# Values of an attention kernel by one indirect gather per unit, with four neighbouring keys to a partition

## The chip, the core and the metric

The kernel runs on one core of a Trainium2 chip. The metric is the device time of the whole launch in microseconds (us); lower is better. Engines are named as the profile names them: PE is the tensor engine's matmul, PEld its weight load, DVE the vector engine, ACT the scalar engine, POOL the GpSimd engine, and SP the engine that issues most of the DMAs (DMAs are issued by ACT and POOL too).

## The reference, cut to what matters

Two layers are added to a residual stream `x` of 8 sequences of 128 tokens and 512 features. Layer 0 is one product per sequence with a weight picked by id. Layer 1 is attention over a paged cache.

```
x = x + einsum('bsi,boi->bso', x, weight[adapter_ids])         # layer 0
# layer 1: 8 sequences, 8 key heads, 4 query heads to a key head, D = 128
q, k, v = x @ Wq.T, x @ Wk.T, x @ Wv.T                          # q and k: RMS norm, rotary angles
kc = k_cache[block_table].reshape(bsz, 512, HK, D)              # 16 pages of 32 keys per sequence
vc = v_cache[block_table].reshape(bsz, 512, HK, D)
k_all, v_all = concat([kc, k]), concat([vc, v])                 # 512 cached keys + 128 new ones
valid_c = arange(512)[None, :] < cache_seqlens[:, None]
probs = softmax(where(valid, q @ k_all.T * SCALE, -1e30))
x = x + (probs @ v_all) @ Wo.T
```

The softmax and the product with the values sum over all keys, so the order in which a unit's 512 cached keys stand is free, as long as scores, mask and values use the same one.

## The kernel before

All of it is one program written by hand for five instruction streams that meet by semaphores; no scheduler orders anything. The work of layer 1 is cut into 64 **units** `u = 8 * hk + b`, one key head `hk` and one sequence `b` each. A unit projects queries (tile `Q`, 128x512), new keys and values (`KV`), turns them, forms the scores of four heads against 640 keys (`S`), takes the softmax, turns the probabilities, multiplies them with the values (`O`), and multiplies the result with the output weights (`Y`). Every fp32 operand is split into a high part (rounded to fp32r) and a low part (the rest), and each product is three matmuls: high x high, low x high, high x low. So each operand has a pair of tiles: `qh`/`ql`, `kh`/`kl` (keys), `vh`/`vl` (values), `wh`/`wl` (weights), `pth`/`ptl` (turned probabilities), `oh`/`ol` (outputs).

The units are pipelined. In **period** `i` the engines work on the scores of unit `i`, the projections of unit `j = i + 1`, the probabilities and values of unit `w = i - 1` and the output product of unit `o = i - 2`. The first loop (`i` from -1 to `NA` = 8) turns probabilities on PE. In the second loop (`i` from 9) they are written as two fp16 planes and turned by DMA transposes that SP issues (`turn_upper`, `turn_lower`).

POOL's stream in a period of the second loop is, in this order: `split_w(i, 0)` (a low part of a 128x512 chunk of weights, tile `wl`, if the table `LO_POOL` has one there), `keys_lo(j)` (tile `kl`), `q_sum(j)` (tile `m`, after DVE's products), `values_hi(w)` (`vh`), `scales(j)` (`var`, `rst`), `values_lo(w)` (`vl`), three `p_lo` (`ptl`), `split_w(i, 1)`, two more `p_lo`. Ten chunks of `wl` fall into eight periods: `LO_POOL` places them so that between two `q_sum` there are 2, 2, 0, 1, 1, 2, 2 and 0 of them, over and over. PE needs `q_sum(j)` for `turn_q(j)` and `p_lo(w, t)` for `times_v(w, t)`, and its own stream is in a fixed order as well.

The cache comes as one array `kv`, with 16 rows of heads (values in the even ones, keys in the odd ones) of 64 pages of 4096 numbers. There, a page of values is 32 keys of 128 numbers; a page of keys is 128 features of 32 keys. For the first nine units (`NL` = 9) keys are loaded page by page from `kv` (`load_kt`), and values by four indirect gathers on POOL (`gather_v`), each of which brings 128 rows of 512 bytes by the row numbers in `kidx` (`kidx1` for unit 8). Meanwhile SP and ACT copy the pages of the later units to `cache_rows` in DRAM, in the order of each sequence's table, 14 rows of heads to a page (12 for sequence 0; `copy_page`, lines 335 to 340; in the periods up to 13). From unit 9 on, `load_k` and `load_v` bring a unit's keys and values from there by one DMA each (lines 342 to 350, and 438 to 445):

```
e.wait_ge(g_vlo, v - 1 if v <= NA else v)
e.dma_start(rawv[raw_at(v)], copy[2 * hk, b].rearrange(
    "k (r d) -> (k r) d", d=D).rearrange("(t p) d -> p t d", p=P)
```

Key number `128 * t + p` stands in partition `p`, tile `t`. SP issues `load_v(i)` in period `i`, after the mask and the weights and ahead of `turn_upper(i, 0)`; it waits until `values_lo(i - 1)` has read the buffer. `keys_hi` (ACT, line 770) rounds the loaded keys into `kh`, `keys_lo` (POOL, line 609) subtracts that from them into `kl`; both read 512 numbers in a row. On DVE, `key_rows` and `key_rows_1` compute the row numbers of the gathers.

## Time and profile before

| | |
|---|---|
| time, median of 3 runs | 1002.83 us (1002.82 to 1006.3) |
| span of the profiled execution | 1006.6 us |
| PE busy | 994.3 us, 99% |
| DVE, ACT, POOL busy | 861.5 (86%), 810.3 (80%), 795.8 us (79%) |
| chain that ended last | PE 95%, DVE 2%, ACTq 1%, ACT 1%, issue 1% |
| moved by DMA | 180.94 MB, 105.45 MB of it read from HBM and 31.86 MB written |
| q1, the queue of most DMAs | 68.9% of the 16 engines |

The page gives no time of its own for the profiled execution beside its span; of the three times listed, the 1006.3 us is the one near it. A share of busy time is a mean over the whole span: the first loop (up to about 190 us) has another mix than the second. In the tables of the trace, a row with an arrow names the tile written and the tiles read, and the bracket at a row's end is how long the engine sat idle before it and what released it.

### The profile page before, as it was taken

The numbers are of one execution on the slowest core, as the hardware profiler recorded it, in microseconds if no ns is written. First come the engines' busy times: TensorE is split into PE (matmuls) and PEld (weight loads), VectorE is DVE, ScalarE is ACT, GpSimd is POOL, SyncE is SP. The second block draws the span as 40 slices with busy tenths as digits, with TensorE's granted clock in tenths as the row PEclk, the third lists the DMA queues.
The fourth block names the chain that finished last, engine by engine and source line by source line (L and its number), as shares of the span: only waits on it lengthen the run. The fifth ranks groups of instructions, "written<-read, shape, count | busy, mean of one in ns | idle before, by whom it ended". The sixth has DMA issues, their size and how long they took to land.

```text
span 1006.6 us, 19441 instructions
## 1 busy us (share of the span) xinstructions
PE 994.3 (99%) x5471; PEld 864.3 (86%) x5471; DVE 861.5 (86%) x1787; ACT 810.3 (80%) x2109; POOL 795.8 (79%) x811
## 2 busy tenths in 40 slices
PE   8999999999999999999999999999999999999998
PEld 6778888888888888888888888888888888888886
DVE  7676657799999899999998999899999999998995
ACT  4455456698889889888988898898888988988884
POOL 4876677497889879897898888898798978888672
PEclk9999999999999999999999999999999999999999
DMA  8999879899988888888988888888988879888873
GB/s 254 277 262 260 283 229 258 213 211 201 221 162 162 161 158 153 166 157 152 171 153 162 156 160 165 148 168 155 170 148 165 157 151 166 162 162 144 153 149 84
DMA packets 513643, 180.94 MB, mean 180 GB/s; under 512 B 429873, under 2 KB 495682, under 8 KB 513538
## 3 DMA queue, kind: packets, MB, share of 16 engines
q1 hardware_dynamic: 381280, 143.20, 68.9%
q10 hardware_dynamic: 131106, 34.15, 15.3%
q0 software_dynamic: 1152, 2.36, 0.8%
q8 instruction: 45, 0.74, 0.3%
q14 instruction: 60, 0.49, 0.2%
HBM read 105.45 MB, written 31.86 MB: 136 GB/s over the span
## 4 chain that ended last, share of the span: by engine, by line
PE 95%; DVE 2%; ACTq 1%; issue 1%; ACT 1%; another core or an unknown queue 0%; POOL 0%; DVEq 0%
PE S L1408 22%; PE O L1341 7%; PE O L1343 7%; PE O L1342 7%; PE Q L1341 6%; PE Q L1343 6%; PE Y L1341 6%; PE Q L1342 6%; PE Y L1343 6%; PE Y L1342 6%; PE T L1347 4%; PE KV L1342 3%; PE KV L1341 3%; PE KV L1343 3%; PE KV L1361 1%; PE Y L1361 1%
## 5 line engine op out<-in xcount | busy, mean ns | idle before, releaser
L1080 DVE SCALAR_TENSOR_TENSOR pr<-pr,rc,raw 128x640 f16<-128x640 f32 x220 | 258.8, 1177 | 15.3 <-ACT raw L817 8.3
L1052 DVE CUSTOM_DVE_ANT_0 pr<-S,mask,rst 128x640 f32<-128x640 f32 x256 | 225.4, 881 | 16.6 <-PE S L1408 13.3
L837 ACT ACTIVATE pr<-pr,nb 128x640 f32<-128x640 f32 x256 | 211.7, 827 | 14.5 <-DVE nb L1052 14.5
L817 ACT ACTIVATE raw<-pr,rc 128x640 f16<-128x640 f32 x220 | 176.2, 826 | 0.6 <-DVE rc L1068 0.4
L617 POOL TENSOR_TENSOR m<-m 128x512 f32<-128x512 f32 x63 | 112.5, 1786 | 73.7 <-DVE m L1119 69.8
L591 POOL TENSOR_SCALAR ptl<-first 128x512 fp32r<-128x512 f16 x140 | 111.8, 799 | 17.6 <-issue 6.0
L570 POOL TENSOR_TENSOR kl<-raw,kh 128x512 fp32r<-128x512 f32 x64 | 97.8, 1528 | 34.5 <-ACT kh L720 33.5
L1408 PE MATMUL S<-kh,qh 128*128 128x320 f32 x512 | 120.8, 317 | 3.7 <-DVE nb L1052 3.6
L591 POOL TENSOR_SCALAR ptl<-turned 128x512 fp32r<-128x512 f16 x135 | 108.3, 802 | 11.2
L1408 PE MATMUL S<-kh,ql 128*128 128x320 f32 x512 | 116.8, 309 | 0.0
L783 ACT ACTIVATE Q<-Q 128x128 f32<-128x128 f32 x256 | 68.2, 266 | 59.9 <-DVE m L1119 59.9
L1408 PE MATMUL S<-kl,qh 128*128 128x320 f32 x512 | 116.2, 308 | 0.0
L1408 PEld LDWEIGHTS S<-kh,qh 128*128 128x128 f32 x512 | 91.7, 189 | 23.8 <-issue 4.7
L1341 PE MATMUL O<-pth,vh 128*128 128x512 f32 x252 | 105.5, 419 | 0.8 <-DVE ptl L983 0.5
L1341 PE MATMUL Y<-wh,oh 128*128 128x512 f32 x252 | 104.7, 415 | 0.4 <-DVE ol L983 0.4
L1341 PE MATMUL Q<-wh,xh 128*128 128x512 f32 x256 | 101.5, 396 | 0.5 <-issue 0.5
L1343 PE MATMUL Q<-wh,xl 128*128 128x512 f32 x256 | 100.9, 394 | 0.0
L1342 PE MATMUL Q<-wl,xh 128*128 128x512 f32 x256 | 100.2, 391 | 0.0
L1342 PE MATMUL Y<-wl,oh 128*128 128x512 f32 x252 | 99.7, 395 | 0.0
L1343 PE MATMUL Y<-wh,ol 128*128 128x512 f32 x252 | 99.6, 395 | 0.0
L1343 PE MATMUL O<-pth,vl 128*128 128x512 f32 x252 | 99.2, 394 | 0.0
L1342 PE MATMUL O<-ptl,vh 128*128 128x512 f32 x252 | 98.6, 391 | 0.0
(179 smaller groups left out, 2674.9 us busy)
## 6 DMA issues: line engine op xcount, KB each, us to landing
wraw<-in_wall SPq DMA_DIRECT2D x74, 256.0 KB, 4.4
cache_rows<-in_kv ACTq DMA_DIRECT2D x80, 224.0 KB
raw<-cache_rows SPq DMA_DIRECT2D x57, 256.0 KB, 4.0
raw<-cache_rows ACTq DMA_DIRECT2D x53, 256.0 KB, 5.0
mask<-mask_rows SPq DMA_DIRECT2D x64, 128.0 KB
cache_rows<-in_kv SPq DMA_DIRECT2D x36, 224.0 KB
first<-in_lw SPq DMA_DIRECT2D x5, 1024.0 KB
cache_rows<-in_kv SPq DMA_DIRECT2D x16, 192.0 KB, 4.2
```

Of the source, the lines that this page charges most:

```text
L570: return e.tensor_tensor(dst, src, hi.bitcast(F32), ALU.subtract)
L591: e.tensor_scalar(ptl[:, i % 3, :].rearrange("p (g n) -> p g n", g=G), plane_tile(u, 1, t), 1.0 / PS, 1.0, ALU.mult, ALU.mult).then_inc(g_ ...
L617: e.tensor_tensor(m1[:, :, :], m1[:, :, :], m2[:, :, :], ALU.add).then_inc(q_added, 1)
L783: made = e.activation(part, part, ACT.Square, accum_out=ssq[:, j % 2, r:r + 1])
L817: e.activation(upper16[:, g, :], pr[:, slot(u, g), :], ACT.Copy, scale=rc[:, u % 2, g:g + 1]).then_inc(a_f1, 1)
L837: e.activation(pr[:, slot(u, g), :], pr[:, slot(u, g), :], ACT.Exp, bias=nb[:, u % 2, g:g + 1], scale=-1.0, accum_out=sm[:, u % 2, g:g + 1 ...
L1052: e.tensor_tensor_reduce(pr[:, slot(u, g), :].rearrange("p (a n) -> p a n", a=2), S[:, :, 0:320], mask[:, u % 2, :].rearrange("p (a n) -> ...
L1080: e.scalar_tensor_tensor(out=lower16(u, g), in0=pr[:, slot(u, g), :], scalar=rc[:, u % 2, g:g + 1], in1=upper16[:, g, :], op0=ALU.mult, op ...
L1341: e.matmul(dst, lh, rh, start=first, stop=False)
L1342: e.matmul(dst, lh, rl, start=False, stop=False)
L1343: return e.matmul(dst, ll, rh, start=False, stop=last)
L1408: made = e.matmul(S[:, a, 0:320], l[:, u % 2, qs], r[:, u % 2, 320 * a:320 * a + 320], start=first, stop=last)
```

## The change

The keys are laid out otherwise: four neighbouring keys stand in one partition. Partition `p` holds keys `4 * (p % 8)` to `4 * (p % 8) + 3` of the unit's page `p // 8`, and tile `t` holds the `t`-th of each four.

- **Values.** The array is split in two, `kc` and `vc`. In `vc` a row is four neighbouring keys, 512 numbers (2 KB). A unit's values are then 128 such rows, one to a partition, and one indirect gather brings them. `gather_v(v)` on POOL does so for all 64 units; `load_v` on SP is gone. In the first loop it stands behind `values_lo(i)`, one gather where there were four; in the second loop it stands at the end of POOL's period, behind `p_lo(w, 4)`, for unit `i`. `values_hi` waits for its semaphore.
- **Row numbers.** `kidx` has one number per partition and unit (64 columns); DVE computes them for one head at a time (`value_rows`), head 0 in the prologue, two heads in each of periods 1 to 3 and the last in period 4. The table comes by one DMA of 128x8 where there were four of 32x32.
- **Copies.** `cache_rows` holds keys alone: `copy_page` moves 7 rows of heads (6 for sequence 0) where it moved 14 (12). The number of copies and their places stay.
- **Keys.** A page of keys is stored with its 32 keys in the order (t, j), key `4 * j + t`. `keys_hi` and `keys_lo` read the loaded keys through a view (`by_tile`) whose runs are 8 numbers long, 64 of them, and write in the order (t, page, j). The mask's numbers (`iota`) stand in the same order.

```diff
-def build(nc, x, xt, lw, wall, kv, ids_lens, table, pages, qkw, consts, iota, out):
+def build(nc, x, xt, lw, wall, kc, vc, ids_lens, table, pages, qkw, consts, iota, out):
...
+        def by_tile(keys):
+
+            return keys.rearrange("d (g t j) -> d t g j", g=NPG, t=NT)
+
+        def tiles_of(keys):
+            return keys.rearrange("d (t g j) -> d t g j", g=NPG, t=NT)
...
-            rows = slice(2 if b >= NL - NB else 4, 2 * NK)
+            rows = slice(1 if b >= NL - NB else 2, NK)
             e.dma_start(copy[rows, b, k, :].rearrange("r (s n) -> s r n", s=16),
-                        kv[rows, bass.ds(number, 1), :].rearrange("r a (s n) -> (a s) r n", s=16)
+                        kc[rows, bass.ds(number, 1), :].rearrange("r a (s n) -> (a s) r n", s=16)
...
-            def load_v(v):
-                hk, b = divmod(v, NB)
-                if v < NL + NB:
-                    e.wait_ge(d_copy[b], 16 * NPG)
-                e.wait_ge(g_vlo, v - 1 if v <= NA else v)
-                e.dma_start(rawv[raw_at(v)], copy[2 * hk, b].rearrange(
-                    "k (r d) -> (k r) d", d=D).rearrange("(t p) d -> p t d", p=P)
-                            ).then_inc(d_v[v % 2], 16)
...
-                if NL <= i < NU:
-                    load_v(i)
...
-            def gather_v(v, t):
-                hk, b = divmod(v, NB)
-                if t == 0:
-                    e.wait_ge(c_kidx, 1)
-                    if hk == 1:
-                        e.wait_ge(c_kidx1, 1)
-                    if v >= 2:
-                        e.wait_ge(g_vlo, v - 1)
-                rows_of = (kidx, kidx1)[hk]
+            def gather_v(v):
+                e.wait_ge(c_kidx, v // NB + 1)
+                if v >= 2:
+                    e.wait_ge(g_vlo, v - 1 if v <= NA else v)
                 e.indirect_dma_start(
-                    out=rawv[raw_at(v)][:, t, :], out_offset=None,
-                    in_=kv.rearrange("c a (r d) -> (c a r) d", d=D),
-                    in_offset=bass.IndirectOffsetOnAxis(
-                        ap=rows_of[:, NT * b + t:NT * b + t + 1], axis=0)
+                    out=rawv[raw_at(v)].rearrange("p t d -> p (t d)"), out_offset=None, in_=vc,
+                    in_offset=bass.IndirectOffsetOnAxis(ap=kidx[:, v:v + 1], axis=0)
                 ).then_inc(d_rawv[v % 2], 16)
...
             def values_hi(u):
-                if u < NL:
-                    e.wait_ge(d_rawv[u % 2], 64 * (u // 2 + 1))
-                else:
-                    e.wait_ge(d_v[u % 2], 16 * ((u - NL) // 2 + 1))
+                e.wait_ge(d_rawv[u % 2], 16 * (u // 2 + 1))
...
-                minus(kl[:, j % 2, 0:512], rawk[raw_at(j)], kh[:, j % 2, 0:512]).then_inc(g_kc, 1)
+                minus(tiles_of(kl[:, j % 2, 0:512]), by_tile(rawk[raw_at(j)]),
+                      tiles_of(kh[:, j % 2, 0:512])).then_inc(g_kc, 1)
...
-                if 1 < j < NL:
-                    gather_v(j, 0)
-                    gather_v(j, 1)
+                if 1 < j <= NA:
+                    gather_v(j)
...
-                if 1 < j < NL:
-                    gather_v(j, 2)
-                    gather_v(j, 3)
...
+                if i < NU:
+                    gather_v(i)
...
-                rounded(kh[:, j % 2, 0:512], rawk[raw_at(j)]).then_inc(a_kc, 1)
+                rounded(tiles_of(kh[:, j % 2, 0:512]), by_tile(rawk[raw_at(j)])).then_inc(a_kc, 1)
...
-            for g in range(4):
-                e.dma_start(tabb[32 * g:32 * g + 32, :],
-                            table[g:g + 1, :].broadcast_to([32, NB * NT])).then_inc(d_tab, 16)
+            e.dma_start(tabb[:, :], table).then_inc(d_tab, 16)
...
-                if i == 2:
-                    key_rows_1()
+                for hk in range(2 * i - 1, 2 * i + 1):
+                    if 1 <= hk < NK:
+                        value_rows(hk)
...
-    iota = np.broadcast_to(np.arange(NT * P, dtype=np.float16), (NB, NT * P))
+    iota = np.broadcast_to(np.arange(NT * P, dtype=np.float16).reshape(P, NT).T.reshape(-1), (NB, NT * P))
...
+        "kc": c(np.asarray(L1_cond_k_cache).reshape(64, ROWS, VK, NK, D).transpose(3, 0, 4, 2, 1).reshape(
+            NK, 64, PSZ * D)),
+        "vc": c(np.asarray(L1_cond_v_cache).transpose(2, 0, 1, 3).reshape(NK * 64 * ROWS, VK * D)),
```

`split_w` and its tables `LO_POOL`, `LO_DVE` and `HI_ACT` are not touched. On POOL, in the second loop, the place where two chunks of `wl` meet in one stretch between two `q_sum` reads so before (`wl` low parts of weights, `kl` of keys, `ptl` of turned probabilities, `m` the query sum, `vh`/`vl` values):

```order
L602 TENSOR_SCALAR vh<-raw 128x512
L632 TENSOR_SCALAR var<-ssq 128x5
L635 TENSOR_TENSOR rst<-var,mhalf 128x5
L570 TENSOR_TENSOR vl<-raw,vh 128x512
L591 TENSOR_SCALAR ptl<-first 128x512 x3
L570 TENSOR_TENSOR wl<-wraw,wh 128x512
L591 TENSOR_SCALAR ptl<-first 128x512 x2
L570 TENSOR_TENSOR wl<-wraw,wh 128x512
L570 TENSOR_TENSOR kl<-raw,kh 128x512
L617 TENSOR_TENSOR m<-m 128x512
```

And so with the change:

```order
L585 TENSOR_SCALAR vh<-raw 128x512
L616 TENSOR_SCALAR var<-ssq 128x5
L619 TENSOR_TENSOR rst<-var,mhalf 128x5
L556 TENSOR_TENSOR vl<-raw,vh 128x512
L577 TENSOR_SCALAR ptl<-first 128x512 x3
L556 TENSOR_TENSOR wl<-wraw,wh 128x512
L577 TENSOR_SCALAR ptl<-first 128x512 x2
L550 DMA raw<-in_vc,kidx 128x512
L556 TENSOR_TENSOR wl<-wraw,wh 128x512
L556 TENSOR_TENSOR kl<-raw,kh 128x512
L601 TENSOR_TENSOR m<-m 128x512
```

One DMA instruction has come in between the last `ptl` of a period and what opens the next one; nothing else moved. On SP, a period of the second loop before:

```order
L486 DMA mask<-mask_rows 128x512
L429 DMA wraw<-in_wall 128x512
L443 DMA raw<-cache_rows 128x4x128
L458 DMA_TRANSPOSE first<-raw 128x10x128
L470 DMA_TRANSPOSE first<-pr 128x10x128
L458 DMA_TRANSPOSE first<-raw 128x10x128
L470 DMA_TRANSPOSE first<-pr 128x10x128
```

And with the change:

```order
L485 DMA mask<-mask_rows 128x512
L437 DMA wraw<-in_wall 128x512
L457 DMA_TRANSPOSE first<-raw 128x10x128
L469 DMA_TRANSPOSE first<-pr 128x10x128
L457 DMA_TRANSPOSE first<-raw 128x10x128
L469 DMA_TRANSPOSE first<-pr 128x10x128
```

The load of the values (L443) is gone from SP's stream.

## Rows read from the trace of the kernel before

**Rows 1.** The page: busy time of each engine, share of the span, instructions
```profile
PE 994.3 (99%) x5471; PEld 864.3 (86%) x5471; DVE 861.5 (86%) x1787; ACT 810.3 (80%) x2109; POOL 795.8 (79%) x811
```

**Rows 2.** Busy time of the engines by stretch; then PEclk, DMA share, GB/s
```profile
25.00:50.00 25.00, 22.94 (x117) 18.16 (x116) 16.41 (x36) 11.21 (x37) 21.92 (x24) 0.93 0.94 278
...
600.00:625.00 25.00, 25.00 (x142) 22.14 (x141) 22.74 (x49) 21.89 (x60) 21.57 (x22) 1.00 0.87 155
```

**Rows 3.** Waits, whole span: waited for, us in total, times, longest
```profile
PE S L1408 <- DVE nb L1052: 3.6, 4, 1.2
...
POOL m L617 <- DVE m L1119: 69.8, 32, 4.6
```

**Rows 4.** Timeline of POOL, second loop: start, us, operation, [idle before, releaser]
```profile
617.63 1.31 POOL L570 TENSOR_TENSOR wl<-wraw,wh 128x512 fp32r<-128x512 f32 x1
618.87 1.91 POOL L570 TENSOR_TENSOR kl<-raw,kh 128x512 fp32r<-128x512 f32 x1
620.89 1.86 POOL L617 TENSOR_TENSOR m<-m 128x512 f32<-128x512 f32 x1
...
623.55 0.20 POOL L632 TENSOR_SCALAR var<-ssq 128x5 f32<-128x5 f32 x1 [0.20 <-ACT KV L788]
...
626.36 2.47 POOL L591 TENSOR_SCALAR ptl<-turned 128x512 fp32r<-128x512 f16 x3
...
635.41 1.87 POOL L617 TENSOR_TENSOR m<-m 128x512 f32<-128x512 f32 x1
...
646.18 1.30 POOL L570 TENSOR_TENSOR kl<-raw,kh 128x512 fp32r<-128x512 f32 x1 [0.94 <-ACT kh L720]
649.82 1.87 POOL L617 TENSOR_TENSOR m<-m 128x512 f32<-128x512 f32 x1 [2.33 <-DVE m L1119]
...
708.00 1.86 POOL L617 TENSOR_TENSOR m<-m 128x512 f32<-128x512 f32 x1 [1.96 <-DVE m L1119]
```

**Rows 5.** Timeline of PE, same period
```profile
622.90 0.45 PE L1408 MATMUL S<-kh,qh 128*128 128x320 f32 x2
...
623.77 0.60 PE L1347 MATMUL T<-ident,m 128*128 128x128 f32 x4
...
629.39 0.40 PE L1341 MATMUL O<-pth,vh 128*128 128x512 f32 x1
```

**Rows 6.** Groups on POOL, by shape: busy us, mean ns, idle before
```profile
L570 POOL TENSOR_TENSOR vl<-raw,vh 128x512 fp32r<-128x512 f32 x64 | 83.1, 1298 | 0.8
...
L562 POOL DMA_INDIRECT raw<-in_kv,kidx x32 | 32.5, 1014 | 18.3 <-DVE kidx L1022 10.7 <-issue 7.5
...
L646 POOL TENSOR_TENSOR tab<-acc 128x384 f32<-128x384 f32 x3 | 3.1, 1023 | 0.0
```

**Rows 7.** Timeline of POOL in the first loop: gathers, and their reader
```profile
16.95 0.95 POOL L562 DMA_INDIRECT raw<-in_kv,kidx  x1 [0.31 <-issue]
...
158.76 0.94 POOL L562 DMA_INDIRECT raw<-in_kv,kidx  x1 [0.30 <-issue]
...
163.59 0.62 POOL L602 TENSOR_SCALAR vh<-raw 128x512 fp32r<-128x512 f32 x1 [0.31 <-DMA raw<-in_kv,kidx]
```

**Rows 8.** Timeline of DVE: prologue, then the period of rows 4
```profile
15.15 2.53 DVE L983 TENSOR_TENSOR wl<-wraw,wh 128x512 fp32r<-128x512 f32 x4
...
618.54 1.07 DVE L1080 SCALAR_TENSOR_TENSOR pr<-pr,rc,raw 128x640 f16<-128x640 f32 x1 [0.36 <-ACT raw L817]
...
620.74 0.87 DVE L1080 SCALAR_TENSOR_TENSOR pr<-pr,rc,raw 128x640 f16<-128x640 f32 x1
621.53 0.87 DVE L1052 CUSTOM_DVE_ANT_0 pr<-S,mask,rst 128x640 f32<-128x640 f32 x1
```

**Rows 9.** Timeline of ACT's issues, prologue; then DMA issues: count, KB, us to landing
```profile
2.56 1.87 ACTq L846 DMA_DIRECT2D tabb<-in_table  x4
...
raw<-cache_rows SPq DMA_DIRECT2D x57, 256.0 KB, 4.0
...
raw<-in_kv,kidx POOLq DMA_INDIRECT x32, 4.7
```

More of the change, by code:

```diff
@@ L519, in _ @@
                     load_k(e, i + 2)
[L520 to L522 removed]
+                for b, t in copies_of(i):
                     copy_pages(b, t)
[L524 to L525 removed]
             for i in range(NA, NU + 2):
@@ L657, in _ @@
             e.wait_ge(c_mhalf, 1)
-            for t in range(NT):
-                gather_v(0, t)
-            for t in range(2):
-                gather_v(1, t)
+            gather_v(0)
+            gather_v(1)
             for i in range(-1, NA + 1):
@@ L1198, in _ @@
             e.tensor_scalar(rnd, rnd, -1.0, HALF_PI, ALU.mult, ALU.add).then_inc(c_ang, 1)
-            key_rows()
+            table_rows()
+            value_rows(0)
             for part in range(2):
```

61 lines of the change are left out of this document (25 added, 36 removed).

## The prediction

> **What bounds the kernel now.** I read the page's busy shares first, then the table by stretch, then the waits, then the timelines of one period. PE is busy 99% of the span [rows 1]. By stretch it is short at the start: from 25 to 50 us it has 22.94 of 25.00, and there the granted clock reads 0.93; in the second loop it has the full 25.00 at clock 1.00 [rows 2]. Its largest wait of the whole run is 3.6 us in four pieces [rows 3]. So nothing that is taken off another engine or off the DMA queues in the middle of the run can shorten it: a period of the second loop is 14.52 us (620.89 to 635.41) [rows 4], all of it PE's. What can change the time is the start, and any engine that has less room in a period than the change takes.
>
> POOL is that engine. Its 79% are a mean over two loops; the timeline tells more. Between two `m` (the query sum) there are two, one or no chunks of `wl`. With none, POOL waits 0.94 us before `kl` and 2.33 before `m`; with one, 1.96 before `m`; with two, `m` shows no wait at all [rows 4]. There, `kl` ends at 620.78 and `m` starts at 620.89, just as its input comes. The stretches repeat as 2, 2, 0, 1, 1, 2, 2, 0: pairs of full ones. Of the 63 `m`, 32 waited for DVE [rows 3]; of the 31 others, 6 are in the first loop and 25 in the second: 12 pairs of full stretches and a single one near its start. So POOL has about 2 us free in most periods and about 0.1 us in the full ones.
>
> **What PE grants POOL.** `m` ends at 622.75, and PE's transpose of it starts at 623.77: 1.0 us of slack. The third `ptl` ends at 626.36 + 2.47 = 628.83, and the matmul that wants it starts at 629.39: 0.56 us [rows 4, 5]. The second is tighter. POOL's own wait of 0.20 us before `var` lies between the two and goes when POOL is late [rows 4], so POOL can be about 0.8 us late before PE stops.
>
> **The change part by part.**
>
> *A gather on POOL in each period of the second loop.* Gathers of 128 rows took 1.014 us on the mean, with 7.5 us of issue gaps over 32 of them, 0.23 each: 1.25 us [rows 6]. The new one also has 128 rows, of 2 KB where these had 512 bytes. No row shows that length. The bounds: 0.95 us, the fastest with nothing behind it [rows 7], and twice the mean with the gap, 2.3 us, if time went partly by bytes. I take 1.25, since the row count is the same and the nearest row is the same operation. In stretches with none or one chunk this lies in waits of 3.27 and 1.96 us [rows 4]: nothing. In a full stretch it makes POOL late.
> First stretch of a pair: 1.25 late at `m`, less the 0.20 before `var`, so 1.05 at the third `ptl`, against 0.56: PE loses 0.5 us. Second stretch: another 1.25, less another 0.20, makes 2.1 us in all, against 0.56: 1.5 us lost by the end of the pair. The stretch behind has no chunk and 3.27 us of waits, so the lateness is gone before the next pair. Sum: 12 x 1.5 + 0.5 = 18.5 us.
>
> *What lies beside the gather.* Two-input operations of POOL and DVE stretch each other: `kl` takes 1.91 us in a full stretch and 1.30 in an empty one, and DVE's `pr<-pr,rc,raw` stands beside it at 618.54 to 619.61 [rows 4, 8]. The gather in the prologue at 16.95 took 0.95 us under DVE's `wl<-wraw,wh`, which also reads two tiles: not stretched [rows 7, 8]. A gather that has slipped under such a DVE row would thus save POOL some 0.6 us (1.91 - 1.30) that a later operation pays now; in the second stretch of a pair that would leave 0.9 us lost instead of 1.5, and 12 x 0.9 + 0.5 = 11 us in all. But the same slip puts `wl` and `kl` against the next DVE row at 620.74, and a DVE row that waits for `kl` is late at `largest` (621.53 to 622.40), which PE wants at 622.90 [rows 5, 8]: up to 0.6 us per full stretch the other way, 25 x 0.6 = 15 us. I take neither and keep both, 11 and 34 us, as ends.
> The Trainium skill (SBUF — State Buffer, "Who interferes with whom") says that a DVE instruction with two SBUF inputs contends with a GpSimd instruction that reads SBUF, not with one that only writes it. By that rule, the sum would be the 11 us, if no DVE row is held up; the row at 16.95 agrees for the gather.
>
> *Strided keys.* `keys_lo` and `keys_hi` read 64 runs of 8 numbers. Six runs of 64 numbers cost nothing visible: 384 elements took 1.023 us where 512 in one run take 1.298 [rows 6]; three quarters of 1.298 is 0.97. If the 0.05 us above that came from 6 runs, 64 would cost 0.5; I take 0, since a fixed cost per instruction explains it as well. At 0.5 us the single stretches (1.96 - 1.25 = 0.7) still fit, and each full one loses 0.5 more: +12 us. ACT is idle 3.1 of 25 us in the second loop [rows 2], so `keys_hi`, once a period, costs nothing.
>
> *The load taken off SP and the queues.* 55 of the 57 issues of `raw<-cache_rows` on SP go [rows 9]; half of each copied page goes. PE waits for none of these: nothing. If they hide anything, it is the DMA transposes, which come in time now. Nothing is gained where PE is full.
>
> *The landing.* A gather is wanted by `vh`. In a full stretch the gather is issued at about 617.7, then come `wl`, `kl`, `m` (1.30 each and 1.2 of stretching), so `vh` is at about 624.0, over 6 us later; in an empty one 645.4 to 651.7, the same. Gathers landed after 4.7 us by the median, with more on the queues than here [rows 9]; one from 158.76 held `vh` until 163.59, 4.8 us [rows 7]. 256 KB take longer than 64 KB; the direct load of as much took 4.0 [rows 9]. I take it as hidden, with 1.3 us to spare.
>
> *The first loop and the start.* POOL issues one gather where it had four, 3 x 1.25 us less per period, where PE is full: nothing. In the prologue ACT issues one table DMA ahead of the weights where it issued four in 1.87 us [rows 9]: 1.4 us earlier at most, but PE's layer-0 product, which SP feeds, must end too before the chain goes on, so I count 0. The seven `value_rows` on DVE are tenths of a microsecond in the first loop, where DVE is busy 16.4 of 25 us [rows 2]: nothing.
>
> **Sum.** 18.5 us on the profiled execution: a span of 1006.6 becomes 1025.1. The profiled one is 3.8 us above the median of the three runs, which I put down to run-to-run spread; on the median, 1002.8 + 18.5 = 1021.
>
> **The rivals.**
> 1. *The lateness is absorbed.* Needed: the gather costs POOL under 0.6 us beside other work, or it falls on DVE's rows in both stretches of a pair (2 x (1.25 - 0.6 - 0.2) = 0.9 late after the second, 0.34 lost, x 12 = 4 us). Against it: in every record of gathers the next operation starts only as the gather ends [rows 7]. It gives 1003 to 1007, no change. This also holds the low end of my own sum.
> 2. *Faster, by the start.* From 25 to 50 us PE is 2.06 us short and at clock 0.93 (1.2 GHz for a part of it; 0.07 x 25 = 1.8 us) [rows 2]. If smaller copies and earlier gathers let PE run through, 3.9 us come back, and 1.4 us from the table DMAs: 5.3 us, so 997.5, provided that POOL's lateness is absorbed too. It decides only if PE's gap there is one of DMA; its longest wait is for DVE's `nb` [rows 3], and POOL's work ahead of it hardly changes. Unlikely.
> 3. *The values land late.* If 256 KB by the gather take 2 us more than the 4.7, 6.7, POOL waits 0.5 us or so in each of 54 periods. In most of them it has the room; in the 25 full ones it costs 0.5 x 25 = 12 more: 1034. At 9 us, 2.5 us more in every period against some 0.7 us of room: 54 x 2 = 108 us, 1110 us. The Trainium skill (DMA: Bandwidth & Descriptors, "Anatomy of one DMA") gives about 2.0 us plus bytes / 436e3, 2.6 us for this size; the trace has 4.7 for a quarter of it.
> 4. *The short runs are dear.* At 0.5 us, 1034 (above). If each of 64 runs cost as much as a small instruction does, microseconds per unit, POOL would be the bound in every period and the time far above 1050. The six-run row speaks against it.
>
> **How the numbers follow.** My forecast (POOL late in full stretches; 11 to 34 us) has 0.62. Rival 1 has 0.17, rival 2 has 0.06, rivals 3 and 4 together 0.15. About 5 us (0.5%) is what a measurement of this kernel can tell from no change, given runs from 1002.8 to 1006.3. Slower by more than that are my forecast and rivals 3 and 4, less a little for their low ends: 0.75; no change 0.19; faster 0.06. The range goes from 1002 (rival 1 inside) to 1042 (the 34 us, and most of rivals 3 and 4's near ends); left out are rival 2 and the dear ends, together under 0.2.
>
> **What would show it.** In the profile after: DMA_INDIRECT on POOL at about 1.0 us, 64 times; `m` without a wait in most periods; PE with waits of 0.3 to 1.3 us for POOL (`m`, `ptl`) or for DVE's `nb` in pairs of periods, none in between; PE short of 25.00 in about every second stretch of the second loop, by 1 to 2 us. Periods of 14.52 us outside the pairs. Right only by accident would be a loss spread evenly over all periods: that would be rival 3 or 4 (`vh` waiting for its DMA, or `kl` well above 1.3 us in empty stretches). Wrong altogether is a PE that stays at 25.00 throughout with POOL busy 55 us more.

## The result, and the profile after

The changed kernel takes **1088.55 us** (median of 4 runs, 1086.75 to 1092.23) where the kernel before takes 1003.4 (4 runs, 1002.82 to 1006.3): a ratio of 1.0843, 95% interval 1.0818 to 1.0869. The forecast was 1021, range 1002 to 1042. The side was right; the time is 67 us above it and outside the range. The profiled execution has a span of 1085.0 us against 1006.6, 78.4 more.

The page's busy shares, after, to be held against [rows 1]:

```profile
PE 1015.5 (94%) x5471; PEld 875.4 (81%) x5471; DVE 959.1 (88%) x1793; ACT 810.9 (75%) x2109; POOL 813.8 (75%) x839
```

PE was busy 994.3 of 1006.6 and is now busy 1015.5 of 1085.0. Its idle time went from 12.3 to 69.5 us, 57.2 more, and its busy time grew by 21.2 us for the same 5471 matmuls; together these are the 78.4. POOL, which I had named as the engine in short supply, grew by 18 us and its share fell. DVE grew by 97.6 us with only 6 instructions more.

The waits of the whole span, after (waited for: us in total, times, longest), beside [rows 3]:

```profile
POOL m L601 <- DVE m L1092: 124.0, 61, 5.9
PE S L1383 <- DVE nb L1025: 57.1, 41, 2.2
PE Q L1316 <- POOL vl L556: 2.8, 1, 2.8
```

Before, PE waited 3.6 us for `nb` and POOL 69.8 us, in 32 of 63 periods, for DVE's `m`. Now PE loses nearly all of its time to `nb`, which DVE's row maximum writes, and POOL waits in 61 of 63 periods. At `m` it is DVE that comes last, not POOL. The groups say where DVE's time went (busy us, mean ns of one, idle before); the kernel before, then after:

```profile
L1080 DVE SCALAR_TENSOR_TENSOR pr<-pr,rc,raw 128x640 f16<-128x640 f32 x220 | 258.8, 1177 | 15.3 <-ACT raw L817 8.3
```

```profile
L1053 DVE SCALAR_TENSOR_TENSOR pr<-pr,rc,raw 128x640 f16<-128x640 f32 x220 | 344.6, 1566 | 10.6 <-ACT raw L794 8.1
L556 POOL TENSOR_TENSOR kl<-raw,kh 128x512 fp32r<-128x512 f32 x64 | 82.3, 1285 | 21.5 <-ACT kh L697 20.6
L550 POOL DMA_INDIRECT raw<-in_vc,kidx x64 | 70.1, 1095 | 27.6 <-issue 13.2 <-DVE kidx L999 10.7 <-PE S L1383 3.7
```

One form, the **score row** `pr<-pr,rc,raw`, took 85.8 of DVE's 97.6 us: the same 220 instructions of the same shape, 1.57 us each instead of 1.18. It reads two tiles of SBUF (`pr` and `raw`). POOL's `kl`, which shared its time with such a row before (1.91 us in a full stretch, [rows 4]), is now always at its undisturbed 1.3 (mean 1.285; 1.528 before). POOL's `kl` got faster, DVE's row slower: the two no longer take turns.

A stretch with two chunks of `wl`, after; POOL, then DVE, then PE (start, us, operation, idle before and its releaser):

```profile
648.00 1.84 POOL L601 TENSOR_TENSOR m<-m 128x512 f32<-128x512 f32 x1 [1.97 <-DVE m L1092]
...
659.32 1.11 POOL L550 DMA_INDIRECT raw<-in_vc,kidx  x1 [0.28 <-issue]
660.46 1.31 POOL L556 TENSOR_TENSOR wl<-wraw,wh 128x512 fp32r<-128x512 f32 x1
661.70 1.30 POOL L556 TENSOR_TENSOR kl<-raw,kh 128x512 fp32r<-128x512 f32 x1
664.97 1.83 POOL L601 TENSOR_TENSOR m<-m 128x512 f32<-128x512 f32 x1 [1.97 <-DVE m L1092]
```

```profile
659.63 4.06 DVE L1053 SCALAR_TENSOR_TENSOR pr<-pr,rc,raw 128x640 f16<-128x640 f32 x1
663.61 0.68 DVE L1088 TENSOR_TENSOR m<-Q,tab 128x512 f32<-128x512 f32 x1
...
664.81 0.87 DVE L1053 SCALAR_TENSOR_TENSOR pr<-pr,rc,raw 128x640 f16<-128x640 f32 x1
665.61 0.87 DVE L1025 CUSTOM_DVE_ANT_0 pr<-S,mask,rst 128x640 f32<-128x640 f32 x1
```

```profile
666.54 0.56 PE L1383 MATMUL S<-kh,qh 128*128 128x320 f32 x2 [2.25 <-DVE nb L1025]
666.94 0.45 PE L1383 MATMUL S<-kl,qh 128*128 128x320 f32 x2
...
668.34 0.63 PE L1317 MATMUL Y<-wl,oh 128*128 128x512 f32 x1
668.77 0.63 PE L1318 MATMUL Y<-wh,ol 128*128 128x512 f32 x1
```

The third row starts at 659.63, 0.31 us into the gather, and lasts until 663.69. POOL's chain gather, `wl`, `kl` ends at 663.00; the row needs some 0.87 us by itself, so it hardly moved before POOL was done (this is inferred from the two ends; no view shows a row's progress). The fourth row, while POOL waits, takes 0.87. Behind the long row stand DVE's two products for `m`, the fourth row and the row maximum; PE waits 2.25 us for that maximum. In the kernel before, the row gets in between `wl` and `kl` and is done after 1.07 us [rows 8].

Behind this stall PE's clock falls. The table by stretch, after (us of PE busy and its matmuls, PEld, DVE, ACT, POOL; PEclk, DMA share, GB/s):

```profile
661.00:666.00 5.00, 3.29 (x22) 2.83 (x20) 5.00 (x5) 1.21 (x10) 3.03 (x3) 1.00 0.64 118
666.00:671.00 5.00, 4.46 (x18) 3.81 (x19) 4.80 (x13) 5.00 (x14) 4.68 (x6) 0.70 0.66 138
```

The granted clock is 0.70 after the stall, that is, 1.2 GHz instead of 2.4 for a good part of those 5 us, and the `Y` matmuls start 0.43 us apart; two `O` matmuls at 655.69 and 655.92 stood 0.23 apart. Over the whole run the clock reads 0.986, against 0.998 before. That is some 13 us (0.014 x 1085.0 less 0.002 x 1006.6) of the 21.2 us of extra busy time. The rest needs no clock: run 6 below has 1018.1 us of PE busy at a clock of 1.000.

Taken over the 53 stretches between two `m` of the second loop, read from the two timelines (length, and duration of the third row, both as means):

| chunks of `wl` in the stretch | count | before | after | loss |
|---|---|---|---|---|
| none | 16 | 14.41 us, row 1.31 | 14.44, row 1.92 | 16 x 0.03 |
| one | 12 | 14.57, row 1.47 | 15.79, row 2.79 | 12 x 1.22 = 15 |
| two | 25 | 14.54, row 1.09 | 16.98, row 3.49 | 25 x 2.44 = 61 |

The sum is 76 of the 78.4 us; the rest is about the wait of 2.8 us above, at the end of the run. In a stretch with one chunk that chunk stands ahead of the period's last two `ptl`, so there, too, only `kl` follows the gather.

One thing holds in all 53 stretches after the change: the third row ends 0.68 to 0.70 us behind the end of `kl`. How long it takes depends only on when it starts. With two chunks it starts 0.3 to 1.9 us behind the gather's start, with one 0.3, with none 1.1 to 1.3. Before, it ended 0.7 behind `kl` with one chunk and with none, but 1.2 us ahead of `kl`'s end with two.

So the 2.44 us of a full stretch (one with two chunks) have two parts. From the start of `m` to the end of `kl` POOL now takes 15.01 us without waiting (648.00 to 663.00 above), 14.43 before: 0.6 is POOL's own lateness. The next `m` follows 1.97 us behind `kl`, where it followed after 0.12: 1.85 is the row that is held until `kl` is done, with DVE's two products behind it. With one chunk `m` follows 1.97 us behind `kl`, as before (1.96), and the whole 1.2 is POOL's lateness, passed on through the row.

Nor does the clock's fall add much time. It shows in eight of the 25 full stretches, whose clock reads 0.90; they are 16.98 us long on the mean, and the 17 at 1.00 are 16.97. PE's next wait is shorter instead: 0.63 us in the stretch after the one shown, 2.22 in others where the clock had stayed up. Once, from 216.09 on, PE's next stretch had no wait to spare (16.29 us, all of it busy), and there the fall cost about 2 us.

### The profile page after: what moved, and what is told of

The parts are those of the page before. It is cut to its first block, busy times and chain, and to the rows that moved or that the text cites. A ratio compares the mean times of both kernels' runs of the same rounds, so it can differ in the third digit from the quotient of the medians.

```text
span 1085.0 us, 19464 instructions
## 1 busy us (share of the span) xinstructions
PE 1015.5 (94%) x5471; PEld 875.4 (81%) x5471; DVE 959.1 (88%) x1793; ACT 810.9 (75%) x2109; POOL 813.8 (75%) x839
## 3 DMA queue, kind: packets, MB, share of 16 engines
HBM read 90.56 MB, written 16.98 MB: 99 GB/s over the span
## 4 chain that ended last, share of the span: by engine, by line
PE 43%; DVE 22%; issue 20%; ACT 12%; DMA 2%; POOL 1%; DVEq 0%; SPq 0%; POOLq 0%; ACTq 0%
PE S L1383 10%; DVE pr L1053 8%; DVE pr L1025 4%; PE T L1322 3%; PE Y L1316 3%; ACT raw L794 3%; PE Y L1317 3%; PE Y L1318 3%; PE O L1316 3%; PE O L1317 3%; PE O L1318 3%; DVE m L1092 2%; PE Q L1316 2%; PE Q L1318 2%; PE Q L1317 2%
## 5 line engine op out<-in xcount | busy, mean ns | idle before, releaser
L1053 DVE SCALAR_TENSOR_TENSOR pr<-pr,rc,raw 128x640 f16<-128x640 f32 x220 | 344.6, 1566 | 10.6 <-ACT raw L794 8.1
L1383 PE MATMUL S<-kh,qh 128*128 128x320 f32 x512 | 125.7, 327 | 57.2 <-DVE nb L1025 57.1
L1316 PE MATMUL Y<-wh,oh 128*128 128x512 f32 x252 | 108.7, 431 | 0.3 <-DVE ol L958 0.3
L1317 PE MATMUL Y<-wl,oh 128*128 128x512 f32 x252 | 102.8, 408 | 0.0
L556 POOL TENSOR_TENSOR kl<-raw,kh 128x512 fp32r<-128x512 f32 x64 | 82.3, 1285 | 21.5 <-ACT kh L697 20.6
```

The costliest lines, as they stand in the source:

```text
L556: return e.tensor_tensor(dst, src, hi.bitcast(F32), ALU.subtract)
L1053: e.scalar_tensor_tensor(out=lower16(u, g), in0=pr[:, slot(u, g), :], scalar=rc[:, u % 2, g:g + 1], in1=upper16[:, g, :], op0=ALU.mult, op ...
L1316: e.matmul(dst, lh, rh, start=first, stop=False)
L1317: e.matmul(dst, lh, rl, start=False, stop=False)
L1383: made = e.matmul(S[:, a, 0:320], l[:, u % 2, qs], r[:, u % 2, 320 * a:320 * a + 320], start=first, stop=last)
```

## The experiments

Theory **A** holds that a gather leaves POOL's parts out of step: some make the gather's descriptors while the others run on into the next instructions, so that POOL, seen as a whole, offers DVE no common gap until it next waits. Rivals were B, that the keys' view with its short runs does it; C, that any instruction of 1.1 us there shifts the phases; D, that the 2 KB rows do. In the diffs, `step` is a tile of one column and `g_step` a semaphore of its own. Runs 1 to 7, 9 and 10 were executed once each; executions of the kernel before lie between 1002.5 and 1008.6 us.

**1. A join behind the gather** (in the changed kernel).

```diff
                     gather_v(i)
+                    e.memset(step[:, :], 0.0).then_inc(g_step, 1)
+                    e.wait_ge(g_step, i - NA)
```

> The changed kernel, but behind each gather of the second loop POOL writes one number per partition and waits until that is done, so that all of POOL is at one point before the next operation. Theory A (the gather occupies only a part of POOL's cores, the others run on into wl and kl, so that POOL's operations leave no common gap in which DVE's two-input rows can read): the long rows of pr<-pr,rc,raw (4.05 us with two chunks, 2.79 with one) fall to below 2 us, and the time falls to 1010 to 1040 us, what POOL's own lateness costs. Theory B (the strided view of the keys is what keeps DVE out) and theory C (any operation of 1.1 us in that place shifts the phases so): no better than the changed kernel, 1085 to 1100 us.

Measured: 1027.48 us (the kernel before on that chip: 1006.95), span 1025.7, clock 0.998. PE's wait for `nb` fell from 57.1 to 11.1 us. A full stretch: POOL, DVE's third row, and the group of the score rows:

```profile
670.60 1.09 POOL L552 DMA_INDIRECT raw<-in_vc,kidx  x1 [0.28 <-issue]
671.70 0.12 POOL L695 MEMSET step<- 128x1 f32 x1
671.90 1.45 POOL L558 TENSOR_TENSOR wl<-wraw,wh 128x512 fp32r<-128x512 f32 x1
```

```profile
671.30 0.88 DVE L1057 SCALAR_TENSOR_TENSOR pr<-pr,rc,raw 128x640 f16<-128x640 f32 x1 [0.34 <-ACT raw L798]
```

```profile
L1057 DVE SCALAR_TENSOR_TENSOR pr<-pr,rc,raw 128x640 f16<-128x640 f32 x220 | 268.2, 1219 | 7.4 <-ACT raw L798 5.6
```

0.12 us of work and a wait of about 0.1 take 61 us off the kernel. The row that lasted 4 us takes 0.88 beside the same gather and the same `wl`. It also does so from the same starting point: in 14 of the 25 full stretches it starts 0.31 to 0.32 us behind the gather's start, as the row of 4.06 did, and takes 0.88 to 0.89.

**2. Keys read straight.** `keys_hi` and `keys_lo` of the changed kernel read and write 512 numbers in a row; the keys are then in another order than values and mask, so that this part of the computation is changed.

```diff
-                minus(tiles_of(kl[:, j % 2, 0:512]), by_tile(rawk[raw_at(j)]),
-                      tiles_of(kh[:, j % 2, 0:512])).then_inc(g_kc, 1)
+                minus(kl[:, j % 2, 0:512], rawk[raw_at(j)], kh[:, j % 2, 0:512]).then_inc(g_kc, 1)
```

> The changed kernel with keys_hi and keys_lo reading 512 numbers in a row again, so that the keys stand in another order than the mask and the values (part of the computation is changed). Theory A and theory C: no change against the changed kernel, 1080 to 1095 us. Theory B: the long DVE rows go, 1005 to 1035 us.

Measured: 1091.39 us, span 1089.6; the row's mean 1594 ns, the group of `kl` 1302 ns against 1285 with the view. B is out, and so is a cost of the short runs.

**3. A filler in the gather's place** (in the kernel before): a small `pow`, 1177 ns by its group.

```diff
                     p_lo(w, 4)
+                if i < NU:
+                    e.tensor_tensor(spare5[:, 0:5], inv_s[:, 0:5], mhalf[:, 0:5], ALU.pow)
```

> The kernel before, with one operation more on POOL in the place of the gather: a power of 128x5 numbers, 1.19 us by the row of rst, worked by all of POOL, whose result nobody reads. Theory A: POOL is late but in step, so only its lateness counts: 1010 to 1035 us, pr<-pr,rc,raw at about 1.2 us on the mean. Theory C: 1070 to 1095 us. Theory B: as theory A, since the keys are read straight here.

Measured: 1017.55 us, span 1015.7, clock 1.0; the row's mean 1275 ns. C is out. In full stretches the third row takes 0.89 us beside the filler. What this lateness alone costs is 9 to 11 us.

**4. A gather of 128 rows of 32 bytes** in that place (in the kernel before, whose values still come by SP; nobody reads what is gathered).

```diff
                     p_lo(w, 4)
+                if i < NU:
+                    if i > NA + 1:
+                        e.wait_ge(d_spare, 16 * (i - NA - 1))
+                    e.indirect_dma_start(
+                        out=spare8[:, :], out_offset=None,
+                        in_=kv.rearrange("c a (r d) -> (c a r) d", d=8),
+                        in_offset=bass.IndirectOffsetOnAxis(ap=kidx[:, 0:1], axis=0)
+                    ).then_inc(d_spare, 16)
```

> The kernel before, with one indirect gather more on POOL in the same place: 128 rows of 32 bytes into a tile that nobody reads. Theory A: the gather alone does it, whatever it moves: 1070 to 1095 us, pr<-pr,rc,raw at 1.5 us on the mean. Theory B, or a cost that goes by the 2 KB rows: 1010 to 1035 us.

Measured: 1082.85 us, span 1081.0, clock 0.986. Its groups and PE's largest wait:

```profile
L1090 DVE SCALAR_TENSOR_TENSOR pr<-pr,rc,raw 128x640 f16<-128x640 f32 x220 | 345.1, 1568 | 10.5 <-ACT raw L827 7.9
L721 POOL DMA_INDIRECT spare<-in_kv,kidx x55 | 60.1, 1092 | 15.4 <-issue 15.2 <-PE S L1418 0.3
```

```profile
PE S L1418 <- DVE nb L1062: 57.3, 41, 2.3
```

One instruction whose result nobody reads gives the kernel before the whole picture of the changed one: 41 waits, 57 us, a row of 1568 ns. A gather of 32-byte rows occupies POOL as long (1092 ns) as one of 2 KB rows (1095). D is out. Against the filler, of nearly the same length and in the same place, the gather costs 65 us more.

**5. The join ahead of the gather** (the two lines of run 1 above `gather_v(i)`).

> The changed kernel with the same small write and wait on POOL as in the run with the join, but ahead of the gather instead of behind it. Theory A (cores out of step behind a gather): no help, since POOL is at one point before the gather and apart behind it; 1080 to 1100 us, the third pr<-pr,rc,raw of a period at about 3.5 us where there are two chunks. Rival (the added operation helped by shifting the phases, or by its wait alone): 1015 to 1040 us.

Measured: 1078.64 us (before: 1006.04), just under A's range; span 1076.7, row mean 1473 ns. Waiting alone does not help; it must be behind the gather. The third row is not as long as A had it, 2.53 us on the mean of the full stretches. In 17 of the 25 it takes 2.67 to 4.05. In the other 8 it starts within 0.2 us of the gather's start and is done in 0.9, and the fourth row is caught instead. POOL, then that row:

```profile
655.69 1.28 POOL L558 TENSOR_TENSOR kl<-raw,kh 128x512 fp32r<-128x512 f32 x1
656.92 1.28 POOL L603 TENSOR_TENSOR m<-m 128x512 f32<-128x512 f32 x1
658.17 0.62 POOL L587 TENSOR_SCALAR vh<-raw 128x512 fp32r<-128x512 f32 x1
658.87 0.66 POOL L618 TENSOR_SCALAR var<-ssq 128x5 f32<-128x5 f32 x1
```

```profile
655.57 3.90 DVE L1057 SCALAR_TENSOR_TENSOR pr<-pr,rc,raw 128x640 f16<-128x640 f32 x1
```

It is kept out through `kl`, `m` and `vh`, which follow each other without a gap, and ends 0.68 us behind `vh`. So it is in seven of the eight; in the last, `vh` waited 0.27 us for its gather, and the row got in ahead of it.

**6. The gather early**, right behind `values_lo`; **7.** the same with the join.

```diff
                 values_lo(w)
+                if i < NU:
+                    gather_v(i)
...
-                if i < NU:
-                    gather_v(i)
```

> The changed kernel with the gather of the second loop right behind values_lo(w), as early as its buffer is free, ahead of the three p_lo. Theory A: POOL is apart from there on until its next wait that blocks, so other DVE rows are hit too (the first and second pr<-pr,rc,raw of a period) and the third still where no wait lies between; 1070 to 1150 us. Rival (it is the nearness of the gather to wl and kl that counts): 1010 to 1040 us.

> As the run before this one, with the join (a small write and a wait for it) behind the gather. Theory A: the DVE rows are short again, and what is left is POOL's lateness at the three p_lo, which PE grants only about 0.6 us: 1.5 late less 0.6, in each of 54 periods, 40 to 50 us less what the later pieces have to spare: 1025 to 1055 us. Rival: no better than the run without the join.

Measured: 1096.32 and 1103.83 us. The busy time of run 6, its largest waits of PE and of POOL for the gather's buffer, and the row:

```profile
PE 1018.1 (93%) x5471; PEld 853.5 (78%) x5471; DVE 863.9 (79%) x1793; ACT 815.0 (74%) x2109; POOL 807.0 (74%) x839
```

```profile
PE O L1316 <- POOL ptl L577: 63.7, 108, 1.3
POOL raw L550 <- POOL vl L556: 40.2, 51, 0.8
```

```profile
L1053 DVE SCALAR_TENSOR_TENSOR pr<-pr,rc,raw 128x640 f16<-128x640 f32 x220 | 234.1, 1064 | 5.6 <-ACT raw L794 5.4
```

At least as slow as the change, for another reason. The row is shorter than in the kernel before (1064 against 1177 ns); the loss is that `ptl` comes later in every period, by the gather's 1.1 us and by 0.8 us in which the gather waits until `vl` has read the buffer. Neither run went as A had it, though the time of run 6 lies in A's range, by accident: run 7 lies 49 us above its range, since I had not counted that wait against the 0.56 us that PE grants there [rows 5]; and in run 6, with `ptl` behind the gather, no row took over 1.9 us, so A had to be amended. The rival of run 7, that the join would bring nothing, came true for the reason that there was no long row to undo.

**8. The change's layout without its gathers in the second loop**: values of units 0 to 8 by one gather each, later ones copied and loaded by SP as before, in rows of 2 KB.

```diff
+                e.dma_start(rawv[raw_at(v)].rearrange("p t d -> p (t d)"),
+                            copy[2 * hk, b].rearrange("k (r n) -> (k r) n", n=VK * D)
+                            ).then_inc(d_v[v % 2], 16)
```

> The layout of the change (four neighbouring keys to a partition, one gather per unit) for the first nine units alone; the pages of keys and values are both copied as before, and from unit 9 on SP loads a unit's values by one DMA, in rows of 2 KB where the kernel before had 512 bytes. No gather in the second loop. Theory A, and the reading that PE bounds the rest: as fast as the kernel before or up to 2 us faster, 1000 to 1004 us. A rival by which the views of the keys or the 2 KB rows cost something of their own: 1006 us or more.

Measured: 1004.87 us (12 runs) against 1006.04 (17 runs), ratio 1.0002, interval 0.9985 to 1.0019. The median lies between the two expectations; by the ratio it is no change. Order of keys, views, table and the single gather of the first loop cost nothing and gain nothing that can be measured. What the change has beyond this run is the second loop's gathers, with smaller copies and without SP's loads, and run 4 has the whole loss from a gather alone.

**9 and 10. How long the effect of a gather lasts.** The small gather of run 4 in the kernel before, at two other places: between the third and the fourth `ptl` (9), and right behind `values_lo` without a wait for it (10).

```diff
                     for t in range(3):
                         p_lo(w, t)
+                if i < NU:
+                    e.indirect_dma_start(
...
                 split_w(i, 1)
```

> The kernel before, with one added gather of 128 rows of 32 bytes per period (to a tile nobody reads), placed between the third and the fourth `ptl` instead of at the end of the period. In both theories POOL is late by the same 1.3 us in the full stretches, worth 10 to 20 us (the filler cost 11). Theory A, strong form (POOL stays apart until it waits): the third score row of DVE meets two `ptl`, wl, kl on a POOL that is apart, so it is as long as with the gather at the end, 3.5 us on the mean in two-chunk stretches; row mean 1.5 us or more, PE waits for `nb` over 45 us, 1065 to 1095 us. Theory A, weak form (being apart wears off within two or three instructions): third row 1.1 to 1.5 us, row mean 1.2 to 1.3 us, 1010 to 1030 us.

> The kernel before, with the same small gather right behind `values_lo`, without waiting for its completion. The three `ptl` come 1.3 us later in every period, against 0.8 us that PE grants: up to 0.5 us x 54 = 27 us as PE waits for `ptl`, plus up to 10 for the full stretches, in either theory: 1020 to 1040 us. Strong form of A: the second or third row of the period, beside `ptl`, wl and kl, is 2 us or more on the mean and PE waits for `nb` on top: over 1060 us. Weak form: row mean near the 1.18 us of before, `nb` waits under 15 us, 1020 to 1045 us.

Measured: 1031.46 us (span 1029.6, row mean 1287 ns) and 1039.11 (span 1037.3, 1086 ns), against 1006.91. PE waits for `nb` 15.2 and 2.5 us, and in run 10 for `ptl` 18.7. Run 9 lies just above the range of the weak form, run 10 within it; both are far from the strong one. In run 9 the second row, beside the gather and the `wl` right behind it, takes 1.80 us on the mean of the full stretches (1.45 before), but the third, beside `wl` and `kl` two `ptl` later, only 1.23. So what the gather sets up ends before POOL waits. The 1.80 is a mean of two kinds, 0.87 us in 13 stretches and 2.7 to 2.84 in 12. One of the long ones, POOL and then the row:

```profile
626.26 1.10 POOL L717 DMA_INDIRECT spare<-in_kv,kidx  x1 [0.28 <-issue]
627.40 1.31 POOL L572 TENSOR_TENSOR wl<-wraw,wh 128x512 fp32r<-128x512 f32 x1
628.79 1.78 POOL L593 TENSOR_SCALAR ptl<-first 128x512 fp32r<-128x512 f16 x2
```

```profile
626.58 2.82 DVE L1090 SCALAR_TENSOR_TENSOR pr<-pr,rc,raw 128x640 f16<-128x640 f32 x1 [0.16 <-ACT raw L827]
```

It ends at 629.40, 0.69 us behind `wl`, just as the third row of the changed kernel ends 0.7 behind a `kl` after which POOL waits. So the row gets in as soon as `ptl` starts, not after it.

**11. The join, and chunks moved.** Run 1 with 26 chunks of `wl` given to DVE, so that POOL has at most one between two `m`.

```diff
+LO_DVE.update({(hk, c): at for hk in range(1, 8) for c, at in ((7, (1, 0)), (9, (2, 0)))})
+LO_DVE.update({(hk, c): at for hk in range(2, 8) for c, at in ((3, (-2, 0)), (4, (-2, 1)))})
```

> The change with the join behind the gather (1027.5 us in its own run), and with the chunks of wl moved so that POOL has at most one between two `m` (the other is DVE's, at places where it has room). If the 20 us that the join leaves are POOL's lateness in stretches with two chunks, they go: 1003 to 1012 us, POOL's m waits for DVE in nearly every period, PE waits for `nb` under 5 us. Rival: DVE, 86% busy before, has no room for 1.3 us more in four of eight periods and is late itself: 1015 to 1035 us, with PE waiting for `nb` or `KV`/`wl` of DVE.

Measured: 1014.75 us (1011.89 to 1017.15), ratio 1.0086, interval 1.0056 to 1.0116. PE waits for `nb` 3.7 us, as before; the 53 stretches take 771.0 us in the profiled execution against 769.1 before and 785.5 in run 1. So the stretches with two chunks were what the join had left. The time is still above the 1003 to 1012 expected, and just under the rival's 1015 to 1035; of that rival's sign, PE waiting for more of DVE, nothing shows. Of the profiled 4.1 us over the kernel before, some 3 are at the end, where the last units follow faster than a gather does:

```profile
972.86 0.62 POOL L589 TENSOR_SCALAR vh<-raw 128x512 fp32r<-128x512 f32 x1 [1.02 <-DMA raw<-in_vc,kidx]
```

```profile
PE Q L1322 <- POOL vl L560: 2.9, 1, 2.9
```

The changed kernel has that wait too (2.8 us once, above); the kernel before has none. The profiled execution is one of the two short ones of the five; what the other three have more, up to 5 us, no trace shows.

**12. The gather one instruction earlier**: no join, nothing added.

```diff
                     p_lo(w, 3)
-                    p_lo(w, 4)
                 if i < NU:
                     gather_v(i)
+                if w < LAST:
+                    p_lo(w, 4)
```

> The change with its gather one instruction earlier: between the period's fourth and fifth `ptl`, so that one operation with a single tensor input (`ptl`, 0.65 us of 128x512 by the group's rows) stands between the gather and wl and kl. Nothing is added; POOL is as late as with the gather at the end. If one such operation (or 0.7 us) behind the gather is enough to bring POOL together again, the third score row of DVE is below 2 us in two-chunk stretches, the row's mean 1.2 to 1.3 us, PE's waits for `nb` 10 to 30 us, and the time 1020 to 1040 us, near the 1027.5 of the join. If it is not enough, the third row stays above 3 us, the waits above 45 us and the time 1070 to 1090. In between (wearing off step by step, as the two runs with the gather still earlier suggest): row 2 to 3 us, 1040 to 1070 us.

Measured: 1033.76 us (1032.85 to 1034.45), ratio 1.0282, interval 1.026 to 1.0303. A full stretch, POOL and then DVE's third row:

```profile
644.09 1.09 POOL L550 DMA_INDIRECT raw<-in_vc,kidx  x1 [0.28 <-issue]
645.25 1.21 POOL L577 TENSOR_SCALAR ptl<-turned 128x512 fp32r<-128x512 f16 x1
646.55 1.29 POOL L556 TENSOR_TENSOR wl<-wraw,wh 128x512 fp32r<-128x512 f32 x1
647.80 1.86 POOL L556 TENSOR_TENSOR kl<-raw,kh 128x512 fp32r<-128x512 f32 x1
```

```profile
645.11 0.89 DVE L1054 SCALAR_TENSOR_TENSOR pr<-pr,rc,raw 128x640 f16<-128x640 f32 x1
```

Two neighbouring instructions changed places, and 55 us are gone. Now `ptl` gives way to the row (1.21 us where an undisturbed one takes 0.62), and `kl` to the next (1.86), as in the kernel before. The third row's mean in full stretches is 0.97 us, where the change has 3.49. The rows start later here, 1.0 to 1.4 us behind the gather's start; but in the change rows that start 1.1 and 1.8 us behind it are held as well. PE's waits for `nb` are 9.3 us. What is left of the loss lies in the full stretches, 15.89 us where the change has 16.98 and the kernel before 14.54: POOL takes 15.94 us to the end of `kl`, and `m` follows at once.

**What is shown and what is not.** Shown: the gather alone does it, with rows of 32 bytes as of 2 KB (4); about the same time of other work does not (3); it is undone by a small write that POOL waits for behind the gather (1), not ahead of it (5), and by one `ptl` between the gather and `wl` (12). The row is held while instructions follow the gather without a gap: one (`kl`, where there is one chunk or none), two (`wl` and `kl`), or, in run 5, `kl`, `m` and `vh`.

Two things bear on the mechanism. The hold sets in while the gather's own record still runs: a row that starts up to 0.17 us behind the gather's start is done in 0.9 us (run 5), and one that starts at 0.31, of which 0.8 us lie beside the gather alone, gets hardly anything done. And it depends on what comes *behind* the gather, since with the join the row that starts at 0.31 is not held. That POOL's parts are out of step, some of them already in `wl`, would do both. It is the picture that led to runs 1 and 5, not something that a row shows. The Trainium skill (Perfetto Trace Analysis, "GPSIMD Engine Instruction") says that POOL is eight DSPs, each with a queue of its own, with "no synchronization between the Q7 DSPs" except within an instruction's implementation, and that the separate queues usually don't matter; in "DMA Instruction — SWDGE (GPSIMD)" it says that two of them make the descriptors of a DMA issued there. By that, the six others would run into `wl` up to 1.1 us ahead of the two, which fits these runs.

Why `ptl` ends it is open. Its single tensor input is not enough as a reason: `vh` has one as well and didn't let the row in (run 5). A wait of 0.7 us is not it either: in run 9 the row got in as `ptl` started. What the traces do show is a gap. In the runs above `ptl` starts 0.06 to 0.09 us behind the end of a gather and 0.08 or more behind a `wl`; `wl` and `kl` start 0.02 to 0.04 behind a gather, and `kl` behind `wl`, as a rule also `vh` behind `m`, with none. With one exception all the rows over 2 us in the change and in runs 2, 4, 5, 9 and 11 end 0.67 to 0.71 us behind a POOL instruction that such a gap, or a wait, follows. In the kernel before, where no gather stands ahead, the row gets in between `wl` and `kl` without such a gap. The gap was not varied by itself.

## Why the prediction was wrong

- **The bound, right.** PE was the bound, the second loop the place, and the single stretch between two `m` the unit in which to count. The losses fall mostly where two chunks meet, 25 times 2.44 us. But I had put the stretches with one chunk at nothing, and they lost 12 times 1.22, 15 us. I read POOL's 1.96 us of waiting before `m` as room. There DVE's row already ended behind `kl`, so `m` came 1.96 us behind `kl` however late `kl` was, and the room was none while the row stayed there. With the change, POOL's 15.01 us and the 1.97 behind them set the length of a full stretch, and PE waits.
- **"A gather on POOL in each period", the price right, the effect small.** I took 1.25 us for one gather; it is 1.095 plus about 0.28 of issue. The row's length did not matter. Lateness of POOL, the one thing in my sum, was forecast at 18.5 us: the filler lost 11.4 us in the second loop, the join 16.3 (spans of the 53 stretches: 780.5 and 785.5 against 769.1), and giving the second chunks away took all but 1.9 of that back. So the term was of the right size, for a kernel in which no row is held.
- **"What lies beside the gather", the step that failed.** I had the two right rows in view: `kl` at 1.91 beside a row of 1.07 [rows 4, 8]. I read them as a fixed stretching of 0.6 us that is paid once by one of the two, and set ends of 11 and 34 us by moving that 0.6 about. What they showed is that the row gets in *between* two POOL instructions: it started at 618.54, during `wl` (617.63 to 618.94), and ended at 619.61, during `kl`. Its price is the time until the next gap. With the gather ahead of `wl` it no longer got in there, and the row took not 0.6 more but 2.4 on the mean of the full stretches and 3 at worst. My largest price for a held-up row was 0.6 us per stretch; it cost 1.85 of the 2.44, the other 0.6 being POOL's lateness. That a DVE row could be held up stood in my upper end, at the price of one stretching; that a gather ahead makes it wait for both instructions behind it was in no term and in no rival.
- **The witness for it was too weak.** I took the gather at 16.95 as "not stretched" under a DVE instruction with two inputs [rows 7, 8]. That says what DVE does to a gather. Nothing in the trace of before had a gather followed at once by a two-input POOL instruction with such a row beside it, so its effect on DVE was not bounded from above by any row. The range had to be open there; a count of the rows that could be caught, 25 stretches with the 2.6 us of `wl` and `kl` behind the gather and 12 with the 1.3 of `kl`, would have given an estimate of 81 us.
- **The Trainium skill's rule.** The Trainium skill's rule on two SBUF inputs (SBUF — State Buffer, "Who interferes with whom") names the right pair, and the trace agrees: DVE's row maximum, `pr<-S,mask,rst`, of the same 128x640 but with one of its two large inputs from PSUM, stays at 878 ns on the mean (881 before), while the score row goes from 1177 to 1566. For the end of 11 us I drew from it that a gather is harmless. By itself it may be; run 4 shows that it is not with `wl` and `kl` behind it.
- **The clock.** No term of the forecast had it. In the second loop it fell to 1.2 GHz, for some 3 us each time, behind 9 of PE's 17 stalls of 2.1 to 2.25 us, and not behind the others. It moved the time by about 2 us only, since PE had waits to spare. In runs 1 and 12 no wait for `nb` is over 1.2 us and the clock reads 0.998 and 1.000.
- **Strided keys, landing, load off SP, the start**: right. `kl` at 1285 ns through the view; gathers of 2 KB rows land after 4.4 us by the median, less than the 4.7 of the 512-byte ones [rows 9]. The first `m` of the second loop starts at 199.14 us where it started at 200.15. One thing escaped me at the end of the run, where units follow faster: POOL waits 1.1, 3.6 and 2.5 us for the last three gathers, and PE 2.8 us once.
- **The rivals.** 1 (absorbed) and 2 (faster by the start) didn't happen. 3 (values land late; its dear end comes to 54 x 1.8 = 97 us, not the 108 that I wrote) is seen in those last three and in one wait of 0.5 us at 234, 4 (short runs) not at all. Of my marks, "PE with waits for DVE's `nb`" was met, but "`m` without a wait in most periods" was the opposite of the 61 waits. Of my forecast only the side came true. The loss is over four times the 18.5 us, and three quarters of what a full stretch lost (1.85 of 2.44) came by a mechanism that the forecast didn't have.

## What to carry to other kernels

Before an instruction is added to POOL beside a DVE that reads two SBUF tiles, look at which gap each such DVE row uses now, and who would fill it; a full POOL costs little here, a POOL that lets DVE in nowhere costs much. Behind an indirect DMA on POOL put something that lets DVE in, here a `ptl` or a tiny write that POOL waits for, and not the next two-input instruction. An engine's wait is room only if what it waits for doesn't itself wait for that engine. When a wait names an engine's small last product (`nb`), go back along that engine to the first instruction that is longer than its twins of the same shape.

## What the runs showed of the hardware that was not expected

- A DVE instruction with two SBUF inputs, 128x640, takes 0.87 us alone, 1.07 when it slips in between two POOL instructions, and 4.06 when it starts 0.3 us into a gather that `wl` and `kl` follow at once. It then ends 0.7 us behind the last of them. A gather of 4 KB in all does this as well as one of 256 KB.
- It is undone by 0.12 us of memset and a wait, or by one `ptl` in between, for 61 and 55 us of the whole.
- A gather of 128 rows occupies POOL for 1.09 us with rows of 32 bytes and of 2 KB alike (1.01 with the 512 bytes of the kernel before, in the first loop).
- Of 17 stalls of PE of 2.1 to 2.25 us, 9 were followed by a fall of the clock. The full stretches with the fall are as long as those without (16.98 and 16.97 us).
